# Zeros written in fixed pieces during attention, the first norm ahead of the memsets, a new order of steps, and a join spread over four engines

## The chip, the cores and the metric

The kernel runs on one core of a Trainium2 chip. The core has five engines that run their own instruction streams and wait for each other by semaphores: TensorE (PE, matmuls; PEld is its weight load), VectorE (DVE), ScalarE (ACT), GpSimd (POOL) and SyncE (SP, which here only issues transfers). Sixteen DMA engines carry out the transfers that SP, ACT and POOL issue. The metric is the device time of one execution in microseconds; lower is better.

## The reference

Inputs are x (32 x 112 x 256), a context (32 x 375 x 256) and the weights of one block. What is computed, cut to what matters:

```python
x = x + tanh(g_xattn) * xattn(layernorm(x), ctx, ctx)      # 16 heads of 16, softmax over 375 keys
x = x + tanh(g_ffn) * ffn(layernorm(x))

def ffn(src):
    x = ln(src + attention(src)) * ln1_g + ln1_b           # 16 heads of 16, over 112 keys
    gates = softmax(x @ gW + gb)                            # 8 experts
    top2_scores, top2_idx = top_k(gates, 2)
    h = relu(x @ W1[e] + b1[e]); y = h @ W2[e] + b2[e]      # F = 512
    return ln(x + sum over the top 2 of score * y) * ln2_g + ln2_b
```

There are 32 items of 112 rows, so 3584 rows. Each row goes to two experts.

## The kernel before, in words

The kernel has three phases on the one core.

**Attention** works on 32 items, each through the stages N (norm of x), A (projections of the context and of x), M (maxima of the scores), B (scores, exp, product with the values), F (output, residual, norm), C, X and D (the same three for the self-attention), and E (output, norm, gate, rank, send). A step such as `B.s1` is a part of a stage. The order of all 1414 steps is written out by hand: `FIRST`, then the list `ORDER` once for each turn from `BEGIN` = 8 to `END` = 26, then `LAST`. `Written.run` walks this one program on every engine, and each engine issues only what it has to do for a step, so the lists are the order in each engine's queue. In `ORDER` a suffix such as `-1` or `+3` shifts the item that the step takes in this turn. Steps that need scores or maxima share one PSUM tensor `quad` (depth 1); most others share three `bank`s. The value tensors `values_A` (3 deep) and `values_C` (2 deep) are set to zero and one by VectorE in `prepare()` (step `S.set`) and, for two of them, ahead of the whole program.

SP issues the loads: `N.load` (x of an item, then its context `ctxT`, each after the slot is free, and then weights that are due), `F.load` (x again, for the residual) and `F.shift` (a store to the DRAM tensor `kept`).

**Routing.** `sent` is a DRAM tensor of 8 regions, one for each expert, of `REGION` = 32 x 112 + 128 rows of 258 numbers. `E.rank` finds for each row the next free places in the regions of its two experts (`next_row` is the count), and `E.send` (POOL, two indirect DMAs for an item) writes the rows there. The experts phase reads whole tiles of 128 rows, so the rows behind the last one of a region must be zero. Before, this was done late: after the ranks of item 29 (`LAST_KNOWN`) VectorE copies the counts to `next_i`, SP reads each of the eight with `value_load` and zeroes the 352 rows behind it (`tails_zeroed`), and the sends of items 30 and 31 wait for that.

**Experts.** VectorE makes a table of tiles (`plan_steps`, `table`), and 63 tiles of 128 rows are loaded from `sent`, pass the two matmuls and are scattered to `kept`. This phase begins on SP when `attention_over` (all sends and stores landed) and the table are there. ACT loads the rows kept for the residual to `x1_in`.

**Join.** 28 tiles of 128 rows: SP loads both expert rows of each (`join_in`, 4 slots), PE adds them into PSUM by two products with the identity, DVE takes bn_stats, bn_aggr and the addition of epsilon, POOL the power -0.5 (`join_inv`), DVE the gain (`join_gain`, one buffer) and the product with the inverse deviation plus the residual (`result`), and ACT issues the store. The plan has 8 written-out turns and a loop of 5 passes of 4.

## Time and profile before

| | |
|---|---|
| median of 3 runs | 1215.42 us (1215.26 to 1216.89) |
| the profiled execution | 1216.49 us, its span 1214.7 us |
| PE busy | 1126.1 us, 93% of the span |
| DVE, ACT, POOL busy | 68%, 57%, 22% |
| granted TensorE clock, mean | 0.98 |
| DMA | 79.18 MB in 66597 packets |

The profiled execution is 1.07 us over the median of the runs. The span runs from the first to the last instruction. Attention takes about the first 910 us, the experts until about 1158, the join the rest. In rows of a timeline the first number is the start in us from the start of the span, the second the length in us; "x8" is how many instructions are merged; what stands in brackets is how long the engine was idle before, and what ended that.

### The profile page before, as it was taken

Reading aid. Unit: us, or ns where it says so; the run is one execution under the profiler, and the core shown is the slowest. Engines: PE = TensorE matmul, PEld = TensorE weight load, DVE = VectorE, ACT = ScalarE, POOL = GpSimd, SP = SyncE. Lnnn points to the kernel's source line nnn. Section 1 sums busy time; section 2 is a strip of 40 time slices with the busy share of each in tenths; the row PEclk is TensorE's granted clock in tenths of the full one; section 3 lists DMA queues with packets and bytes.
Section 4 is the critical chain, followed back from the end, with each engine's and each line's share of the span. In section 5 each row is a group of like instructions: output and inputs, shape, how many; then the busy total and the mean of one; then the engine's idle time right before and its main releaser. Section 6 shows DMA issues by size and latency. Waiting matters only on the chain.

```text
span 1214.7 us, 36448 instructions
## 1 busy us (share of the span) xinstructions
PE 1126.1 (93%) x12924; PEld 840.5 (69%) x12925; DVE 827.8 (68%) x2431; ACT 688.4 (57%) x1186; POOL 265.8 (22%) x371
## 2 busy tenths in 40 slices
PE   6999999999999999999999999999728999999964
PEld 4576766676766666676666677667517999999942
DVE  5565777776777777667777776777744666666667
ACT  4666767677666667777667776776513333333200
POOL 1011111122212111222212221222321222222233
PEclk9999999999999999999999999999968999999988
DMA  6012043222111111111111011101056222222165
GB/s 149 22 42 68 17 123 105 69 68 74 40 33 37 51 34 33 38 41 34 33 53 38 10 45 46 30 28 64 28 116 187 71 69 71 72 72 71 52 212 159
DMA packets 66597, 79.18 MB, mean 65 GB/s; under 512 B 14008, under 2 KB 52536, under 8 KB 66328
## 3 DMA queue, kind: packets, MB, share of 16 engines
q1 hardware_dynamic: 52680, 54.24, 16.2%
q0 software_dynamic: 6096, 15.66, 3.9%
q10 hardware_dynamic: 7680, 7.34, 1.9%
q8 instruction: 95, 1.56, 0.6%
q14 instruction: 46, 0.38, 0.1%
HBM read 51.32 MB, written 25.90 MB: 64 GB/s over the span
## 4 chain that ended last, share of the span: by engine, by line
PE 75%; issue 9%; DVE 8%; ACT 4%; POOL 1%; DMA 1%; DVEq 0%; another core or an unknown queue 0%; SPq 0%; POOLq 0%; ACTq 0%
PE quad L1299 11%; PE bank L1289 10%; PE bank L1485 9%; PE quad L1497 9%; PE quad L1311 8%; PE sums L1322 6%; PE bank L1436 4%; PE bank L1389 4%; ACT probs L777 4%; PE quad L1308 3%; PE bank L1282 3%; PE bank L1457 2%; PE bank L1322 2%; DVE row_max_C L1050 2%; DVE row_max_C L1047 2%
## 5 line engine op out<-in xcount | busy, mean ns | idle before, releaser
L777 ACT ACTIVATE probs<-quad 125x1792 f32<-125x1792 f32 (+1 forms) x128 | 213.0, 1664 | 116.9 <-PE quad L1311 116.7
L855 ACT ACTIVATE scored_half<-quad 112x750 bf16<-112x750 f32 (+1 forms) x160 | 131.4, 821 | 89.5 <-PE quad L1299 89.0
L1037 DVE TENSOR_REDUCE row_max_A<-quad 112x2 f32<-112x750 f32 x128 | 120.1, 938 | 70.0 <-PE quad L1299 66.5
L1485 PE MATMUL bank<-tile_inT,tile_w 128*128 128x128 f32 x1008 | 124.4, 277 | 0.3 <-ACT tile_w L887 0.3
L1039 DVE TENSOR_REDUCE row_max_A<-scored_half 112x2 f32<-112x750 bf16 x128 | 118.6, 927 | 3.2 <-ACT scored_half L855 1.0
L1485 PEld LDWEIGHTS bank<-tile_inT,tile_w 128*128 128x128 f32 x1008 | 119.0, 194 | 0.7 <-ACT tile_w L887 0.7
L1497 PE MATMUL quad<-output_w,hiddenT 128*128 x504 | 119.1, 380 | 0.0
L1299 PE MATMUL quad<-kT_A,qT_A 32*112 32x375 f32 x1024 | 115.2, 519 | 3.5 <-ACT probs L777 1.5
L1216 DVE TENSOR_SCALAR hiddenT<-bank,hidden_b 128x128 f32<-128x128 f32 x252 | 71.0, 344 | 63.0 <-PE bank L1485 62.6
L1289 PE MATMUL bank<-ctxT,wxk 128*128 128x375 f32 x256 | 99.1, 510 | 5.5 <-DMA bxk<-in_bxk_dram 5.5
L739 POOL DMA_INDIRECT kept_dram<-tile_out,take_back x63 | 60.4, 959 | 186.3 <-DVE tile_out L1239 179.7
L1497 PEld LDWEIGHTS quad<-output_w,hiddenT 128*128 128x128 f32 x504 | 90.9, 190 | 10.0 <-issue 0.2
L1389 PE MATMUL bank<-wxv,ctxT 128*125 128x256 f32 x384 | 95.5, 385 | 0.0
L1322 PE MATMUL sums<-probs,values_A 125*32 125x112 f32 x3072 | 92.5, 261 | 0.4 <-issue 0.4
L684 POOL TENSOR_TENSOR inv_std_N<-moments_N,minus_half 112x1 f32<-112x1 f32 x32 | 17.6, 549 | 333.9 <-DVE moments_N L945 333.9
L1311 PE MATMUL quad<-qT_A,kT_A 32*125 32x224 f32 x1536 | 88.8, 347 | 0.0
L725 POOL DMA_INDIRECT sent_dram<-xm,send_row x64 | 61.7, 964 | 104.5 <-DVE send_row L1108 47.3
L1322 PEld LDWEIGHTS sums<-probs,values_A 125*32 125x32 f32 x3072 | 72.0, 109 | 14.1 <-issue 9.0
L1389 PEld LDWEIGHTS bank<-wxv,ctxT 128*125 128x125 f32 x384 | 69.1, 189 | 14.8 <-issue 5.1
L1311 PEld LDWEIGHTS quad<-qT_A,kT_A 32*125 32x125 f32 x1536 | 73.0, 183 | 0.0
L1289 PEld LDWEIGHTS bank<-ctxT,wxk 128*128 128x128 f32 x256 | 44.8, 194 | 37.4 <-issue 21.6
L887 ACT ACTIVATE tile_w<-hidden_w 128x1024 f32 x63 | 66.1, 1049 | 0.0
(225 smaller groups left out, 1995.0 us busy)
## 6 DMA issues: line engine op xcount, KB each, us to landing
ctxT<-in_ctxT_dram SPq DMA_DIRECT2D x32, 375.0 KB, 3.5
tile_in<-sent_dram SPq DMA_DIRECT2D x63, 129.0 KB
join_in<-kept_dram SPq DMA_DIRECT2D x28, 256.0 KB, 3.4
hidden_w<-in_hidden_w_dram SPq DMA_DIRECT2D x8, 512.0 KB, 5.0
output_w<-in_output_w_dram SPq DMA_DIRECT2D x8, 512.0 KB, 5.7
x_in<-in_x_dram SPq DMA_DIRECT2D x32, 112.0 KB, 2.9
x_res<-in_x_dram SPq DMA_DIRECT2D x32, 112.0 KB, 3.2
kept_dram<-x_shift SPq DMA_DIRECT2D x32, 112.0 KB
```

Source lines behind the costliest of these rows:

```text
L777: act.activation(probs[0:rows, t.buffer("probs", step), :, :], quad[0:rows, :, 0:U * T], ACT.Exp, scale=SCALE).then_inc(taken[kind_of(step ...
L855: act.activation(scored_half[:, t.buffer("half", step), 0:RT // 2 * n].rearrange("t (r s) -> t r s", s=n), quad[0:T, RT // 2:RT, 0:n], ACT ...
L1037: dve.tensor_reduce(row_max["A"][:, i:P // 2:ROWS], quad[0:T, 0:RT // 2, 0:S], AX_X, ALU.max).then_inc(taken[kind], 1)
L1039: dve.tensor_reduce(row_max["A"][:, P // 2 + i:P:ROWS], scored_half[:, t.buffer("half", step), 0:RT // 2 * S].rearrange("t (r s) -> t r s" ...
L1216: ins = dve.tensor_scalar(hiddenT[:, k, f, :], hidden_bank[k][:, f * P:(f + 1) * P], hidden_b[:, f, bass.ds(e, 1)], 0.0, ALU.add, ALU.max)
L1289: mm = pe.matmul(out, w[:, c, m * P:(m + 1) * P], actT[:, c, :], start=c == 0, stop=c == DC - 1)
L1299: mm = pe.matmul(quad[0:T, i, at:at + n], qT[a][rows, k, c, e, :], kT[a][rows, k, c, :], start=True, stop=True)
L1311: mm = pe.matmul(quad[0:n, i, c * RH * T:(c + 1) * RH * T], kT[a][rows, k, c, j * n:(j + 1) * n], qT[a][rows, k, c, :, :].rearrange("p e t ...
L1322: mm = pe.matmul(out[h * VW:(h + 1) * VW, g * T:(g + 1) * T], values[a][0:n, k, j, g * G + h, :], probs[0:n, b, i, (c * RH + e) * T:(c * R ...
L1389: mm = pe.matmul(bank[0:SC, (j - first) * D:(j - first + 1) * D], ctxT[:, k, c, j * SC:(j + 1) * SC], wxv[:, c, :], start=c == 0, stop=c = ...
L1485: mm = pe.matmul(hidden_bank[k][:, f * P:(f + 1) * P], tile_w[:, k, c, f * P:(f + 1) * P], tile_inT[:, k, c, :], start=c == 0, stop=c == D ...
L1497: mm = pe.matmul(output_bank[k][:, 0:D], hiddenT[:, k, f, :], output_w[:, f, bass.ds(e * D, D)], start=f == 0, stop=f == FC - 1)
```

## The change

1. **The zeros.** `next_i`, the late zeroing and its wait are gone. SP zeroes all regions in 33 fixed pieces of 112 rows (the last of 128), the same rows of all eight regions at once, in two DMAs each. The pieces go out behind the loads of `N.load` from item 4 on, one or two with each. A send of item n waits until piece n + 1 has landed (the last one until all have).
2. **The first norm.** All memsets of the value rings stand in `prepare()`, and in `FIRST` the step `N.ln` of item 0 stands ahead of `S.set`. The bias `bxk` is loaded ahead of `wxk`.
3. **The order.** `ORDER`, `FIRST` and `LAST` are new. In `ORDER`, `N.load` stands without `+3`, and `F.load` with `+1`.
4. **The join.** The plan is written out for all 28 turns. DVE keeps bn_stats, bn_aggr, the gain (`join_gain` now 4 deep) and one addition of epsilon for two tiles; POOL does one power for two tiles and adds the residual to the result; ACT multiplies by the inverse deviation (`ACT.Copy` with a scale) and stores. `result` is 8 deep. POOL, not DVE, waits for `x1_loaded`.

The steps from X.max to E.aT and from D.s to B.s2 in `ORDER`, before and after (| is the end of a turn):

```
before: ... X.max A.q E.send-2 E.oN A.v0 F.norm-1 E.aT ...   ... D.s | A.k0 M.mT-1 B.s2-1 ...
after:  ... X.max A.q E.oN A.v0 X.mT E.send-1 E.aT ...   ... D.s A.k0+1 E.gate F.load+1 M.mT E.pick B.s2 ...
```

```diff
@@ -46,8 +46,7 @@
 REGION = NB * T + P
 
 
-LAST_KNOWN = NB - 3
-BEHIND = (NB - 1 - LAST_KNOWN) * T + P
+FIRST_CLEAR = 4
 NT = NB * T * TOP // P + E - 1
 
 
@@ -176,48 +175,48 @@
 PROBS = 4
 
 ORDER = [
-    "A.k0", "M.mT-1", "B.s2-1", "D.pv-1", "E.gate-1", "B.pv1-1", "N.ln-1", "E.pick-1", "E.rank-1", "B.pv2-1",
-    "E.copy-2", "B.s0", "A.k1", "F.oN", "A.xT", "X.max", "A.q", "E.send-2", "E.oN", "A.v0", "F.norm-1", "E.aT",
-    "M.max0", "F.aT", "F.res", "E.out", "B.s1", "F.out", "A.v1", "M.max1", "F.shift-1", "C.yT", "B.pv0", "N.load+3",
-    "M.max2", "F.load+3", "C.qk0", "X.mT", "M.max3", "C.qk1", "C.bias-1", "C.v", "E.norm", "D.s"]
+    "F.shift-1", "N.ln-1", "B.pv2-1", "B.s0", "F.oN", "A.xT", "F.norm-1", "A.k1", "X.max", "A.q", "E.oN", "A.v0",
+    "X.mT", "E.send-1", "E.aT", "M.max0", "C.bias-1", "F.aT", "E.out", "B.s1", "F.out", "A.v1", "M.max1", "C.yT",
+    "N.load", "B.pv0", "M.max2", "C.qk0", "C.v", "M.max3", "E.norm", "C.qk1", "F.res+1", "D.s", "A.k0+1", "E.gate",
+    "F.load+1", "M.mT", "E.pick", "B.s2", "E.rank", "E.copy", "D.pv", "B.pv1"]
...
 FIRST = """
-    A.k0 A.xT S.set A.k1 A.q A.v0 N.ln S.mask N.ln M.max0 A.k0 M.max1 M.max2 A.v1 A.xT M.max3 A.k1 A.q N.load M.mT
...
+    A.k0 A.xT N.load N.ln S.mask S.set A.k1 A.q A.k0 N.ln M.max0 M.max1 A.xT A.k1 N.load M.max2 A.q M.max3 A.v0
...
@@ -241,9 +240,11 @@
 JT = NB * T // P
 JR = 4
 
-JOIN = Plan(JT, 8, JR, {"A": 0, "B": 1}, ["A.add", "B.norm"], {})
+RR = 8
+
+JOIN = Plan(JT, JT, 1, {"A": 0, "G": 1, "V": 1, "R": 3, "S": 4}, ["A.add", "G.gain", "V.power", "R.scale", "S.store"], {})
 X1_PARTS = 4
-assert JT % X1_PARTS == 0
+assert JT % X1_PARTS == 0 and JT % 2 == 0
 
@@ -557,15 +556,6 @@
                         keys_over(sp)
                         sp.dma_start(output_b[:, :], io["output_b"].rearrange("e d -> (e d)").partition_broadcast(P)
                                      ).then_inc(output_b_loaded, DMA)
-                    elif step == "E.rank" and t.item("E") == LAST_KNOWN:
-
-                        sp.wait_ge(rows_zeroed, 5)
-                        sp.wait_ge(rows_known, 1)
-                        for e in range(E):
-                            row_no = sp.value_load(next_i[0:1, e:e + 1], min_val=e * REGION, max_val=e * REGION + (LAST_KNOWN + 1) * T)
-                            sp.dma_start(io["sent"][bass.ds(row_no, BEHIND), :].rearrange("(p r) (h d) -> p (r h) d", r=4, h=2),
-                                         zero_row[0:BEHIND // 4, :].unsqueeze(1).to_broadcast([BEHIND // 4, 8, SENT // 2])
-                                         ).then_inc(tails_zeroed, DMA)
                     elif step == "F.shift":
                         n, k = t.item("F"), t.slot("F")
                         sp.wait_ge(shifted, t.item("F", 1, 1))
@@ -573,8 +563,8 @@
 
             def load_weights(stage):
                 if stage == "K":
+                    column(bxk, io["bxk"]).then_inc(w_loaded["K"], DMA)
                     square(wxk, io["wxk"]).then_inc(w_loaded["K"], DMA)
-                    column(bxk, io["bxk"]).then_inc(w_loaded["K"], DMA)
                 if stage == "Q":
                     square(wxq, io["wxq"]).then_inc(w_loaded["Q"], DMA)
                     column(bxq, io["bxq"]).then_inc(w_loaded["Q"], DMA)
@@ -597,11 +587,25 @@
                         row(b, io[a]).then_inc(w_loaded["C"], DMA)
                     sp.dma_start(gate_w[:, :, :], io["gate_w"].rearrange("(c p) e -> p c e", p=P)).then_inc(w_loaded["C"], DMA)
 
+            def clear(j):
+
+                rows = T if j < NB else REGION - NB * T
+                regions = io["sent"][:, :].rearrange("(e r) d -> r e d", e=E)
+                for half in (slice(0, SENT // 2), slice(SENT // 2, SENT)):
+                    sp.dma_start(regions[j * T:j * T + rows, :, half],
+                                 zero_row[0:rows, :].unsqueeze(1).to_broadcast([rows, E, SENT // 2])).then_inc(regions_zeroed, DMA)
+
             def turn(t):
                 move(t)
                 n = t.item("N")
                 if t.only != "N.load":
                     return
+                if n == FIRST_CLEAR:
+                    sp.wait_ge(rows_zeroed, 5)
+                if n >= FIRST_CLEAR:
+                    cleared = [(NB + 1) * m // (NB - FIRST_CLEAR) for m in (n - FIRST_CLEAR, n - FIRST_CLEAR + 1)]
+                    for j in range(*cleared):
+                        clear(j)
                 for stage in ("KQV", "BC")[n] if n < 2 else ():
                     load_weights(stage)
                 if n == 6:
@@ -719,8 +723,7 @@
                         pool.wait_ge(xm_copied, t.item("E", 1, 1))
                         pool.wait_ge(row_steps, t.item("E", 6, 6))
                         settled(pool, passed_pool)
-                        if t.item("E") > LAST_KNOWN:
-                            pool.wait_ge(tails_zeroed, E * DMA)
+                        pool.wait_ge(regions_zeroed, (t.item("E") + 1 if t.item("E") < NB - 1 else NB + 1) * 2 * DMA)
                         for i in range(TOP):
                             pool.indirect_dma_start(out=io["sent"], out_offset=bass.IndirectOffsetOnAxis(
                                 ap=send_row[:, k, i:i + 1], axis=0), in_=xm[:, k, i, :], in_offset=None).then_inc(sent[k], DMA)
@@ -740,15 +743,21 @@
                         ap=take_back[:, k, :], axis=0), in_=tile_out[:, k, :], in_offset=None).then_inc(out_stored[k], DMA)
 
             EXPERTS.run(pool, expert_turn)
+            pool.wait_ge(x1_loaded, X1_PARTS * DMA)
 
             def join_turn(t):
-                if t.active("B"):
-                    k = t.slot("B", JR)
-                    pool.wait_ge(join_steady, t.item("B", 1, 1))
-                    if t.later("B", JR):
-                        pool.wait_ge(result_steps, t.item("B", 2, 2 - 2 * JR))
-                    pool.tensor_tensor(join_inv[:, k, :], join_moments[:, k, 1:2], minus_half[:, :],
-                                       ALU.pow).then_inc(join_inverted, 1)
+                if t.active("V") and t.item("V") % 2:
+                    n, k = t.item("V"), t.slot("V", JR)
+                    pool.wait_ge(join_steady, n // 2 + 1)
+                    if t.later("V", JR):
+                        pool.wait_ge(join_scaled, n - JR + 1)
+                    pool.tensor_tensor(join_inv[:, k - 1:k + 1, :], join_moments[:, k - 1:k + 1, 1:2],
+                                       minus_half[:, :].unsqueeze(1).to_broadcast([P, 2, 1]), ALU.pow).then_inc(join_inverted, 1)
+                if t.active("R"):
+                    n, k = t.item("R"), t.slot("R", RR)
+                    pool.wait_ge(join_scaled, n + 1)
+                    pool.tensor_tensor(result[:, k, :], result[:, k, :], x1_in[:, n * D:(n + 1) * D],
+                                       ALU.add).then_inc(join_summed, 1)
 
             JOIN.run(pool, join_turn)
 
@@ -894,20 +903,29 @@
             EXPERTS.run(act, expert_turn)
 
             def join_turn(t):
-                if t.active("B"):
-                    n, k = t.item("B"), t.slot("B", JR)
-                    act.wait_ge(result_steps, t.item("B", 2, 2))
-                    act.dma_start(io["out"][bass.ds(n * P, P), :], result[:, k, :]).then_inc(result_stored[k], DMA)
+                if t.active("R"):
+                    n, k = t.item("R"), t.slot("R", RR)
+                    act.wait_ge(join_inverted, n // 2 + 1)
+                    act.wait_ge(join_gained, n + 1)
+                    if t.later("R", RR):
+                        act.wait_ge(result_stored[k], t.dmas("R", 0, depth=RR))
+                    act.activation(result[:, k, :], join_gain[:, t.slot("R", JR), :], ACT.Copy,
+                                   scale=join_inv[:, t.slot("R", JR), :]).then_inc(join_scaled, 1)
+                if t.active("S"):
+                    n, k = t.item("S"), t.slot("S", RR)
+                    act.wait_ge(join_summed, n + 1)
+                    act.dma_start(io["out"][n * P:(n + 1) * P, :], result[:, k, :]).then_inc(result_stored[k], DMA)
 
             JOIN.run(act, join_turn)
-            for k in range(JR):
-                act.wait_ge(result_stored[k], JT // JR * DMA)
+            for k in range(RR):
+                act.wait_ge(result_stored[k], (JT - k + RR - 1) // RR * DMA)
 
         @block.vector
         def _(dve):
             def prepare():
 
-                dve.memset(values["A"][:, DEEP["A"] - 1, :, :, :], 0.0).then_inc(vset, 1)
+                for i in range(DEEP["A"]):
+                    dve.memset(values["A"][:, i, :, :, :], 0.0).then_inc(vset, 1)
                 for k in range(DEEP["C"]):
                     dve.memset(values["C"][:, k, :, :, :], 0.0).then_inc(vset, 1)
                 dve.wait_ge(vset, DEEP["A"] + DEEP["C"])
@@ -1106,8 +1124,6 @@
                         dve.tensor_reduce(route[:, 0:TOP], rows_pick[:, :, :], AX_X, ALU.add).then_inc(row_steps, 1)
                         dve.wait_ge(row_steps, t.item("E", 6, 5))
                         dve.tensor_copy(send_row[:, k, :], route[:, 0:TOP]).then_inc(row_steps, 1)
-                        if t.item("E") == LAST_KNOWN:
-                            dve.tensor_copy(next_i[:, :], next_row[:, :]).then_inc(rows_known, 1)
                     elif step == "F.out":
                         dve.wait_ge(made["F.out"], t.count(step))
                         dve.wait_ge(res_shifted, t.item("F", 1, 1))
@@ -1160,8 +1176,6 @@
                         dve.scalar_tensor_tensor(xm[:, k, 0, 0:D], r_gain[:, :], inv_std["E"][:, :], ln1_b[0:T, :],
                                                  ALU.mult, ALU.add).then_inc(gained, 1)
 
-            for i in range(DEEP["A"] - 1):
-                dve.memset(values["A"][:, i, :, :, :], 0.0).then_inc(vset, 1)
             ATTENTION.run(dve, turn)
             keys_over(dve)
 
@@ -1240,36 +1254,30 @@
 
             EXPERTS.run(dve, expert_turn)
 
-            dve.wait_ge(x1_loaded, X1_PARTS * DMA)
-
             def join_turn(t):
-                a, b = t.active("A"), t.active("B")
-                kA, kB = t.slot("A", JR), t.slot("B", JR)
-                if a:
-                    dve.wait_ge(join_added, t.item("A", 1, 1))
+                n, k = t.item("A"), t.slot("A", JR)
+                if t.active("A"):
+                    dve.wait_ge(join_added, n + 1)
                     if t.later("A", 2):
-                        dve.wait_ge(join_measured, t.item("A", 2, -2))
-                    dve.bn_stats(join_stats[:, t.slot("A"), :], join_bank[kA][:, 0:D]).then_inc(join_measured, 1)
-                if b:
-                    if t.later("B", 1):
-                        dve.wait_ge(result_steps, t.item("B", 2))
-                    dve.scalar_tensor_tensor(join_gain[:, :], join_bank[kB][:, 0:D], join_moments[:, kB, 0:1], ln2_gain[:, :],
-                                             ALU.subtract, ALU.mult).then_inc(result_steps, 1)
-                if a:
-                    dve.wait_ge(join_measured, t.item("A", 2, 1))
+                        dve.wait_ge(join_measured, 2 * n - 2)
+                    dve.bn_stats(join_stats[:, t.slot("A"), :], join_bank[k][:, 0:D]).then_inc(join_measured, 1)
+                if t.active("G"):
+                    m, km = t.item("G"), t.slot("G", JR)
+                    dve.wait_ge(join_measured, 2 * m + 2)
+                    if t.later("G", JR):
+                        dve.wait_ge(join_scaled, m - JR + 1)
+                    dve.scalar_tensor_tensor(join_gain[:, km, :], join_bank[km][:, 0:D], join_moments[:, km, 0:1], ln2_gain[:, :],
+                                             ALU.subtract, ALU.mult).then_inc(join_gained, 1)
+                if t.active("A"):
+                    dve.wait_ge(join_measured, 2 * n + 1)
                     if t.later("A", JR):
-                        dve.wait_ge(result_steps, t.item("A", 2, 2 - 2 * JR))
-                    settled(dve, passed_dve)
-                    dve.bn_aggr(join_moments[:, kA, :], join_stats[:, t.slot("A"), :]).then_inc(join_measured, 1)
-                    dve.wait_ge(join_measured, t.item("A", 2, 2))
-                    dve.tensor_scalar(join_moments[:, kA, 1:2], join_moments[:, kA, 1:2], TOP * TOP * EPS, None, ALU.add).then_inc(join_steady, 1)
-                if b:
-                    dve.wait_ge(result_steps, t.item("B", 2, 1))
-                    dve.wait_ge(join_inverted, t.item("B", 1, 1))
-                    if t.later("B", JR):
-                        dve.wait_ge(result_stored[kB], t.dmas("B", 0, depth=JR))
-                    dve.scalar_tensor_tensor(result[:, kB, :], join_gain[:, :], join_inv[:, kB, :], x1_in[:, bass.ds(t.item("B", D), D)],
-                                             ALU.mult, ALU.add).then_inc(result_steps, 1)
+                        dve.wait_ge(join_gained, n - JR + 1)
+                        dve.wait_ge(join_inverted, (n - JR) // 2 + 1)
+                    dve.bn_aggr(join_moments[:, k, :], join_stats[:, t.slot("A"), :]).then_inc(join_measured, 1)
+                    if n % 2:
+                        dve.wait_ge(join_measured, 2 * n + 2)
+                        dve.tensor_scalar(join_moments[:, k - 1:k + 1, 1:2], join_moments[:, k - 1:k + 1, 1:2], TOP * TOP * EPS, None,
+                                          ALU.add).then_inc(join_steady, 1)
 
             JOIN.run(dve, join_turn)
 
```

The rest of the diff declares the tensors and semaphores that these lines name, drops `next_i` and its copy and the memsets after `prepare()`, moves all `values_A` memsets into `prepare()`, and lets PE wait for `join_gained` before it reuses a bank in the join.

## Rows read from the trace of the kernel before

**Rows 1.** Windows: us, busy us (instructions) by engine, granted clock, DMA share, GB/s.
```profile
0.00:25.00 25.00, 16.48 (x70) 9.55 (x72) 14.57 (x35) 8.97 (x18) 3.91 (x26) 1.00 0.71 157
400.00:500.00 100.00, 98.22 (x1314) 69.12 (x1313) 70.90 (x199) 70.03 (x122) 22.45 (x32) 1.00 0.12 34
850.00:900.00 50.00, 29.96 (x381) 21.67 (x380) 36.24 (x157) 20.75 (x52) 13.25 (x18) 0.87 0.31 69
900.00:940.00 40.00, 24.04 (x156) 21.71 (x157) 12.05 (x45) 9.24 (x14) 7.67 (x8) 0.74 0.56 164
```

**Rows 2.** Timeline of the head: start, length, engine, line, operation, idle before.
```profile
1.17 1.34 DVE L1164 MEMSET values_A<- 125x1536 f32 x1 [1.04 <-PEq L1536]
...
5.50 2.84 PE L1289 MATMUL bank<-ctxT,wxk 128*128 128x375 f32 x4 [5.50 <-DMA bxk<-in_bxk_dram]
...
10.30 0.63 PE L1282 MATMUL bank<-ident,x_norm 112*128 112x112 f32 x2 [1.96 <-DVE x_norm L950]
...
18.34 0.94 DVE L1037 TENSOR_REDUCE row_max_A<-quad 112x2 f32<-112x750 f32 x1 [5.28 <-PE quad L1299]
```

**Rows 3.** Waits of PE, 100 to 840 us: total, times, longest.
```profile
PE quad L1308 <- ACT probs L777: 4.3, 18, 0.3
PE bank L1282 <- DVE att_E L962: 3.9, 18, 0.4
```

**Rows 4.** Timeline of the seam between attention and experts.
```profile
878.43 22.21 SPq L566 DMA_DIRECT2D sent_dram<-zero_row  x8
...
897.35 0.17 DVE L1108 CAST send_row<-route 112x2 uint32<-112x2 f32 x1
...
900.34 0.28 DVE L1203 CAST table<-bank 1x126 int32<-1x126 f32 x1 [0.46 <-PE bank L1464]
...
905.96 0.98 POOL L725 DMA_INDIRECT sent_dram<-xm,send_row  x1 [11.90 <-DMA sent_dram<-zero_row]
...
909.73 0.94 POOL L725 DMA_INDIRECT sent_dram<-xm,send_row  x1 [0.30 <-issue]
913.35 29.20 SPq L631 DMA_DIRECT2D tile_in<-sent_dram  x11
```

**Rows 5.** Windows of the join: written-out turns, then the loop.
```profile
1168.30:1175.46 7.16, 5.19 (x22) 3.45 (x20) 6.99 (x27) 0.00 (x0) 3.69 (x6) 1.00 0.97 315
1175.46:1203.80 28.34, 19.43 (x70) 12.05 (x71) 24.67 (x85) 0.00 (x0) 11.27 (x18) 1.00 0.77 230
```

**Rows 6.** Timeline of the join: tile 3's turn, and the end.
```profile
1168.30 0.42 DVE L1252 BATCH_NORM_STATS2 join_stats<-sums 128x6 f32<-128x256 f32 x1
...
1168.64 0.47 DVE L1256 SCALAR_TENSOR_TENSOR join_gain<-bank,join_moments,ln_gain 128x256 f32<-128x256 f32 x1
1169.03 0.17 DVE L1263 BATCH_NORM_AGGREGATE join_moments<-join_stats 128x2 f32<-128x6 f32 x1
1169.23 0.15 DVE L1265 TENSOR_SCALAR join_moments<-join_moments 128x1 f32<-128x1 f32 x1
1169.31 0.49 DVE L1271 SCALAR_TENSOR_TENSOR result<-join_gain,join_inv,x_in 128x256 f32<-128x256 f32 x1
1169.46 0.74 POOL L750 TENSOR_TENSOR join_inv<-join_moments,minus_half 128x1 f32<-128x1 f32 x1 [0.67 <-DVE join_moments L1265]
...
1207.38 0.42 DVE L1252 BATCH_NORM_STATS2 join_stats<-sums 128x6 f32<-128x256 f32 x1
...
1209.57 0.49 DVE L1271 SCALAR_TENSOR_TENSOR result<-join_gain,join_inv,x_in 128x256 f32<-128x256 f32 x1
```

**Rows 7.** DMA queues, 876 to 906 us: packets, MB, share of 16 engines.
```profile
q1 hardware_dynamic: 5848, 3.02, 48.9%
```

**Rows 8.** DMA issues of the page: count, KB each, us to landing.
```profile
ctxT<-in_ctxT_dram SPq DMA_DIRECT2D x32, 375.0 KB, 3.5
```

**Rows 9.** Groups by line and shape, GpSimd and ScalarE: count, busy, mean ns.
```profile
L714 POOL TENSOR_TENSOR y_bias<-y,bso 112x256 f32<-112x256 f32 x32 | 23.4, 732 | 10.0 <-DVE y L950 10.0
...
L841 ACT ACTIVATE xm<-xm 112x256 f32<-112x256 f32 x32 | 13.0, 410 | 4.8 <-DVE xm L1160 4.8
```

82 lines of the change are left out of this document (40 added, 42 removed).

## The prediction

> **What bounds the kernel now.** I read the windows first: busy time of each engine in stretches that follow the stages. In the middle of attention TensorE is busy 98.22 of 100 us at the full clock, no other engine over 71 [rows 1]: there TensorE's work sets the pace, and an edit can win only the 1.8% between its instructions. TensorE stands idle at three places: 8.5 us in the first 25; the end of attention with the start of the experts, where 850 to 940 us hold 54 us of work, 36 idle [rows 1]; and the join, where it waits for VectorE. So I read the timeline of those three, and the waits of TensorE for the stretch between.
>
> *Head.* TensorE starts at 5.50, when the bias bxk lands, needs 2.84 us for the first keys, and then waits 1.96 for x_norm: VectorE had begun with the memsets of the value rings at 1.17, and the first norm stood behind them [rows 2].
>
> *Middle.* Two waits make up most of its gaps, each once in each of the 18 written-out turns: 4.3 us for the probabilities and 3.9 for att_E [rows 3].
>
> *Seam to the experts.* The last rows to send are known at 897.35, and the table at 900.62. But GpSimd's send waits 11.90 us for the zeros behind the rows, whose eight DMAs SyncE issues from 878.43 to 900.64, each after reading its place from next_i; four sends then run from 905.96 to 910.67 and the first expert tile is fetched at 913.35 [rows 4]. The wait lies on the chain.
>
> *Join.* VectorE is busy 6.99 of 7.16 us in the written-out turns, while the DMA engines are at 0.97 and move 315 GB/s [rows 5]. One turn is five instructions, 0.42, 0.47, 0.17, 0.15 and 0.49 us long [rows 6]. In the loop the turn is longer: tile 3's bn_stats starts at 1168.30 and tile 27's at 1207.38, 39.08/24 = 1.63 us a tile, with DMA at 0.77 and 230 GB/s [rows 5, 6].
>
> **The change, part by part.** *1. The tails' zeroing goes away.* Sends then wait for pieces zeroed long before: piece n+1 leaves with an input load some four turns ahead of send n. The two sends of tile 31 need send_row (897.35 + 0.17); with one handoff they start near 897.7 and, at the spacing of the four, (909.73 - 905.96)/3 = 1.26 us [rows 4], the last starts at 898.96 instead of 909.73: **-10.8**. Tile 30's two sends, ready at about 890, fit in before. Next late is the table at 900.62; the last send lands by 898.96 + (913.35 - 909.73) = 902.6, so the table costs nothing. Bounds: -9.5 if table and a queue for GpSimd cost 1.3 more, -11.3 with nothing between.
>
> *2. The zeros during attention.* 33 pieces, two DMAs each, 896 runs of 516 bytes in each. Before, 5,632 such packets made up nearly all of 5,848 on that queue, which took 48.9% of 16 engines' 30 us: 235/5848 = 40 ns each [rows 7]. A piece is 1,792 x 40 ns / 16 = 4.5 us of all engines, about one in a turn of 27 us, while the DMA share there is 0.12 [rows 1]. SyncE issues eight of 704 runs in 22 us with the reads between [rows 4], so at most 2.8 us for each, 6 to 7 us a turn, after the turn's own loads. Behind the zeros stand F.load, F.shift and the next N.load. In the 18 turns these have over 10 us of spare TensorE work ahead of their use, by counting the steps between. In the hand-written end there is less: the context of item 26 and the x of item 30 leave about one landing (3.5 us for ctxT [rows 8]) before use. I take **+1** for it, bounds 0 and +6 (one piece, 4.5, and a part of a second ahead of such a load).
>
> *3. First norm ahead of the memsets.* x_norm is then ready before the first keys are done: the 1.96 us go. But the memsets now stand ahead of M.max0, which VectorE did at 18.34 after being idle 5.28 [rows 2]; the work that moved is longer than that idleness by little. bxk issued before wxk only swaps which lands last. **-1.5**, bounds 0 and -3.
>
> *4. The new order.* Between D.s and the next B.s2 stand the same two steps (A.k0, M.mT) in both, so the 4.3 us stay. Between E.oN and E.aT the new order puts X.mT as well, 0.25 us of TensorE, against a wait of 3.9/18 = 0.22 a turn: up to -3.9 [rows 3]. FIRST and LAST leave a little less work between some users of the one quad (M.max, B.s); by counting, 1 to 2 us more. After B.pv2 of the last item, both orders hold nearly the same steps, so the chain to the last send stays as long. **-2.0**; all the 8.2 us of waits are too much, so the bounds are -5 and, for a tight place that I don't see, +5.
>
> *5. The join.* VectorE loses the last product (0.49) and half of the small additions (0.15 each); from start to start in rows 6, bn_stats to gain takes 0.34, gain to bn_aggr 0.39, bn_aggr 0.17 and a handoff, and every second turn the addition with its wait, 0.28 at most: about 1.05 a tile. ScalarE gets a scaling like its copy of 112x256, 0.41, and the store. GpSimd gets the addition of 112x256, 0.73 [rows 9], and one power for two tiles, 0.74 [rows 6]: (0.74 + 2 x 0.73)/2 = 1.1, with three handoffs of 0.1 to 0.15 some 1.25. The DMA engines move 256 KB in and 128 KB out for a tile, 393 kB: at 315/0.97 = 325 GB/s that is 1.21 us, at 230/0.77 = 299 it is 1.31 [rows 5]. So the bound passes from VectorE to the DMA engines and GpSimd together: 1.28 a tile, 24 x (1.63 - 1.28) = -8.4. The end gets longer: one result now passes power, two scalings, an addition on GpSimd and the store. From tile 27's bn_stats to its store it was 2.7 us; it is 0.34 + 0.39 + 0.2 + 0.2 for VectorE, 0.85 for the power, 0.9 for two scalings, 0.85 for the sum, 3.9 with handoffs: +1.2. **-7.2**; bounds: at 1.21 a tile -8.9, at 1.57 (below) +0.3.
>
> In rows 6 the power on GpSimd takes 0.74 while a product with two SBUF inputs runs on VectorE, and the new join has no such product left. The Trainium skill (SBUF — State Buffer, "SBUF: two separate sides") says that GpSimd and VectorE lock their shared pair exclusively when VectorE has two SBUF inputs or a 2-port mode; by it the new additions are disturbed less. The Trainium skill (GPSIMD Engine Reference, "Performance versus the Vector engine") also holds that an addition of two tensors is 1.96 times VectorE's; on VectorE's product of 0.47 that would be an estimate of 0.92 for one, 1.3 us a tile for GpSimd and -6.6 for this part; the row has 0.73.
>
> **Sum.** -10.8 + 1.0 - 1.5 - 2.0 - 7.2 = -20.5 us. The profiled execution took 1216.49, so 1196.0; it is 1.07 over the median of the runs, so **1195** against 1215.42.
>
> **Rivals.**
> - *The join gains nothing*: GpSimd becomes its bound. If each addition is held by VectorE's gain (0.47), a pair is 0.74 + 2 x (0.73 + 0.47) = 3.1, 1.57 a tile, 24 x 0.06 = 1.4 less 1.2 for the end: 1202. For it: GpSimd's power, a single column, takes 0.74 beside VectorE's products [rows 6]. Against: the 0.73 is measured in attention, with VectorE at 71% [rows 1, 9]. 15%.
> - *Everything works*: the order wins its 3.9 and more, head -3, join at 1.21: 1188. 15%.
> - *Order or zeros cost*: a tight place in the 18 turns, 0.3 us each (+5), or GpSimd and VectorE held by a late load near item 30: 1200 to 1204. 10%.
> - *The other side, slower than before*: the zeros delay loads in every turn. N.load stands in its own turn now, no longer three ahead, and waits in SyncE's queue behind F.shift and the zeros before. Were TensorE held in each of the 28 loads, the change turns slower from 20.5/28 = 0.73 us each; by a full piece (4.5 us) it would be 1215.4 - 21.5 + 126 = 1320. Against: the load leaves about a turn before use, and ctxT lands 3.5 us after issue [rows 8]. 5%, of which 2 for a delay that just eats the gain.
> - *The zeros weren't on the chain* (something else ends at 910): the wait of 11.90 names them, and SyncE's reads end at 900.64; 1206. 4%.
>
> **How the numbers follow.** 51% for 1195 with its own range 1191 to 1199; with the rivals at 1188 and 1202 on the two sides, 1187 to 1205 leaves out the 5%, the 4% and the ends of the others. Within 0.2% (2.4 us, about what a measurement of this kernel can tell from no change) 2%; slower 3%; faster 95%.
>
> **What the profile after would show.** No wait of GpSimd for zeros near 900, and the first tile_in about 3.5 us after the last send_row plus two sends, near 902.6 on the old time base (some 3 us earlier by head and order). The wait of 1.96 for x_norm gone. In the middle TensorE at 98.2 to 98.6 of 100 and DMA share 0.28 to 0.34 instead of 0.12. In the join, bn_stats of tiles 3 and 27 about 30.7 us apart, VectorE busy near 80%, DMA share over 0.9, GpSimd over 80%. Wrong would be: a wait of TensorE or VectorE for ctxT or x_in; a turn longer than before; a join at 1.4 us and more, with the additions over 0.9 us.

## The result, and the profile after

The changed kernel took **1222.55 us** (median of 20 runs, 1216.11 to 1233.85) against 1215.10 us (20 runs, 1213.66 to 1216.89) of the kernel before beside it: ratio 1.0062, 95% interval 1.0044 to 1.0080. That is slower by 0.6%; I had predicted 1195 us. Its profiled execution took 1223.01 us, with a span of 1220.8. Its line numbers are 3 to 18 higher than before. Of the experiments further down, one of the four runs of long_runs_again was slow (1604.64 us, mean granted clock 0.65): the median in its row holds it, its ratio does not.

First the two ends, since they came out nearly as predicted. The seam, timeline, against [rows 4]:

```profile
918.68 0.17 DVE L1126 CAST send_row<-route 112x2 uint32<-112x2 f32 x1
919.67 0.94 POOL L728 DMA_INDIRECT sent_dram<-xm,send_row  x1 [1.90 <-DVE send_row L1126]
920.91 0.94 POOL L728 DMA_INDIRECT sent_dram<-xm,send_row  x1 [0.30 <-issue]
921.76 0.28 DVE L1217 CAST table<-bank 1x126 int32<-1x126 f32 x1 [0.46 <-PE bank L1472]
924.62 1.52 SPq L635 DMA_DIRECT2D tile_in<-sent_dram  x2
```

From the last send_row to the first expert tile it is now 924.62 - 918.68 = 5.94 us, before 913.35 - 897.35 = 16.00: -10.06. The wait for the zeros is gone. The join, against [rows 5, 6], the bn_stats of tiles 3 and 27 and a window between:

```profile
1180.34 0.43 DVE L1263 BATCH_NORM_STATS2 join_stats<-sums 128x6 f32<-128x256 f32 x1 [0.22 <-PE sums L1519]
...
1210.76 0.43 DVE L1263 BATCH_NORM_STATS2 join_stats<-sums 128x6 f32<-128x256 f32 x1
```

```profile
1185.00:1205.00 20.00, 15.27 (x62) 10.42 (x61) 14.49 (x54) 8.12 (x16) 16.53 (x25) 1.00 0.96 310
```

24 tiles take 30.42 us instead of 39.08. VectorE is busy 72% of the time and GpSimd 83%; the DMA share is 0.96. So the bound did pass to the transfers, with GpSimd close behind. From tile 27 to the end it is 10.04 us, before 7.32.

But the last send_row comes at 918.68, not at 897.35: all that the ends won was lost, and more, before it. The windows, against [rows 1] (in the two stretches from 100 to 300, which have no row there, TensorE was busy 98.60 and 98.15 of 100 us before):

```profile
0.00:25.00 25.00, 16.33 (x70) 8.74 (x72) 14.46 (x35) 9.25 (x20) 3.91 (x26) 0.93 0.71 160
100.00:200.00 100.00, 92.27 (x1232) 64.33 (x1231) 69.04 (x170) 65.19 (x111) 18.11 (x26) 0.97 0.59 112
200.00:300.00 100.00, 92.46 (x1146) 65.50 (x1147) 61.66 (x163) 62.25 (x108) 19.11 (x27) 0.93 0.54 106
400.00:500.00 100.00, 99.30 (x1296) 69.87 (x1293) 73.50 (x186) 71.29 (x127) 23.05 (x32) 1.00 0.34 72
```

Where nothing disturbs it, as from 400 to 500, TensorE is busy 99.3 of 100 us, better than I forecast (98.2 to 98.6). From 100 to 300 it is idle 15 us, and the granted clock is 0.97 and 0.93. The waits of TensorE from 100 to 840 us, against [rows 3]:

```profile
PE sums L1330 <- issue: 9.5, 3, 4.2
PE quad L1307 <- ACT probs L786: 5.3, 4, 3.0
PE quad L1316 <- ACT probs L786: 4.2, 18, 0.2
PE quad L1319 <- issue: 2.5, 1, 2.5
```

The wait for att_E is gone, and the 4.2 us for the probabilities are there as predicted. New are waits for "issue": time in which the engine stood still, though nothing that the profile shows was missing. One of them, in the timeline of TensorE, falls into the middle of a group of 16 matmuls with the same inputs:

```profile
261.65 0.72 PE L1319 MATMUL quad<-qT_A,kT_A 32*125 32x224 f32 x9
...
264.83 1.12 PE L1319 MATMUL quad<-qT_A,kT_A 32*125 32x224 f32 x7 [2.46 <-issue]
```

No operand can be late between the ninth and the tenth. Another one, at 507, stops two engines at once, with the windows around it:

```profile
510.98 1.66 ACT L786 ACTIVATE probs<-quad 125x1792 f32<-125x1792 f32 x1 [3.82 <-remote]
511.04 0.26 DVE L978 RECIPROCAL inv_sum_F<-bank 112x16 f32<-112x16 f32 x1 [3.98 <-remote]
...
512.70 1.05 PE L1307 MATMUL quad<-kT_C,qT_C 32*112 32x112 f32 x32 [3.00 <-ACT probs L786]
```

```profile
503.00:506.00 3.00, 3.00 (x106) 2.50 (x102) 2.37 (x13) 2.63 (x7) 0.00 (x0) 1.00 1.24 139
506.00:509.00 3.00, 3.00 (x53) 2.29 (x44) 0.41 (x1) 0.80 (x2) 2.46 (x4) 1.00 1.24 186
509.00:512.00 3.00, 0.69 (x3) 0.09 (x1) 0.93 (x3) 1.02 (x1) 1.26 (x2) 1.00 0.40 91
512.00:515.00 3.00, 2.31 (x39) 2.20 (x40) 1.26 (x3) 2.27 (x4) 0.00 (x0) 0.83 0.02 5
```

Four DMAs of zeros (two pieces) had been issued together, from 495.97 on. The share of the DMA engines is 1.24 up to 509, and they move only 139 and 186 GB/s, where they moved 310 in the join. ACT and DVE come back 2 us after the share begins to fall, at 509. The granted clock then is 0.83 in the mean of the next window, that is, the lower level, 1.2 GHz, for a part of it: the idle stretch costs twice. From 100 to 840 us the clock is at the lower level for 23.8 us in all, in the trace of late_zeros_third below never. In these 740 us the waits for issue add up to 14.2 us and the waits of L1307 for the probabilities to 4.8 more than there; the 23.8 us at half the clock cost up to 11.9 more, an estimate. The other long turns lie at the same kinds of places: where a piece leaves with 1 MB of expert weights (items 6 to 13), or where two pieces leave together.

The page's DMA queues, against 66597 packets and a queue q1 of 16.2% before:

```profile
q1 hardware_dynamic: 107408, 81.99, 32.7%
...
q8 instruction: 96, 1.57, 0.6%
```

### The profile page after: what moved, and what is told of

It reads as the page before. It is cut to its first block, busy times and chain, and to the rows that moved or that the text cites. A ratio compares the mean times of both kernels' runs of the same rounds, so it can differ in the third digit from the quotient of the medians.

```text
span 1220.8 us, 36170 instructions
## 1 busy us (share of the span) xinstructions
PE 1134.5 (93%) x12924; PEld 849.9 (70%) x12925; DVE 821.4 (67%) x2388; ACT 707.8 (58%) x1214; POOL 276.9 (23%) x385
## 3 DMA queue, kind: packets, MB, share of 16 engines
q1 hardware_dynamic: 107408, 81.99, 32.7%
q8 instruction: 96, 1.57, 0.6%
## 4 chain that ended last, share of the span: by engine, by line
PE 85%; ACT 4%; issue 4%; DMA 2%; DVE 2%; POOL 1%; another core or an unknown queue 1%; SPq 0%; POOLq 0%; DVEq 0%; ACTq 0%
PE bank L1297 12%; PE quad L1307 11%; PE bank L1493 9%; PE quad L1505 9%; PE quad L1319 8%; PE bank L1397 7%; PE sums L1330 7%; PE bank L1444 5%; PE quad L1316 4%; ACT probs L786 3%; PE bank L1290 3%; PE bank L1433 3%; PE bank L1465 2%; PE bank L1330 2%; DMA join_in<-kept_dram 2%
## 5 line engine op out<-in xcount | busy, mean ns | idle before, releaser
L1307 PE MATMUL quad<-kT_A,qT_A 32*112 32x375 f32 x1024 | 115.7, 521 | 5.6 <-DVE row_max_A L1055 4.4
L1319 PE MATMUL quad<-qT_A,kT_A 32*125 32x224 f32 x1536 | 91.6, 355 | 2.5 <-issue 2.5
L688 POOL TENSOR_TENSOR inv_std_E<-moments_E,minus_half 112x1 f32<-112x1 f32 x32 | 18.8, 589 | 235.1 <-DVE moments_E L963 234.9
```

The costliest lines, as they stand in the source:

```text
L1307: mm = pe.matmul(quad[0:T, i, at:at + n], qT[a][rows, k, c, e, :], kT[a][rows, k, c, :], start=True, stop=True)
L1319: mm = pe.matmul(quad[0:n, i, c * RH * T:(c + 1) * RH * T], kT[a][rows, k, c, j * n:(j + 1) * n], qT[a][rows, k, c, :, :].rearrange("p e t ...
```

## The experiments

My theory after this (A): the bursts of small packets keep the engines from getting their instructions. Rivals: the new order is slower (B); loads come late behind the zeros (C); the bytes or the total, not the burst of packets, cost (D). The ratio is always to the kernel before on the same chip. It takes 1203.9 us (medians 1203.85 to 1204.34) beside the first, third and fourth group of experiments, and 1216.6 beside the second.

| kernel | us | ratio, 95% interval | kernel before |
|---|---|---|---|
| late_zeros | 1203.59 | 0.9998 (0.9988 to 1.0007) | 1203.89 |
| zeros_in_before | 1214.49 | 1.0089 (1.0072 to 1.0106) | 1203.89 |
| apart | 1212.62 | 1.0071 (1.0055 to 1.0088) | 1203.89 |
| long_runs | 1190.12 | 0.9883 (0.9866 to 0.9899) | 1203.89 |
| after_again | 1220.95 | 1.0041 (1.0027 to 1.0055) | 1216.62 |
| join_only | 1210.20 | 0.9944 (0.9927 to 0.9961) | 1216.62 |
| long_old_order | 1201.97 | 0.9884 (0.9867 to 0.9900) | 1216.62 |
| long_runs_again | 1191.21 | 0.9876 (0.9856 to 0.9896) | 1203.85 |
| late_zeros_again | 1204.12 | 1.0000 (0.9990 to 1.0010) | 1203.85 |
| long_quads | 1205.42 | 1.0013 (0.9995 to 1.0031) | 1203.85 |
| after_third | 1212.22 | 1.0073 (1.0049 to 1.0097) | 1204.34 |
| late_zeros_third | 1204.47 | 1.0002 (0.9993 to 1.0012) | 1204.34 |
| long_runs_third | 1189.83 | 0.9884 (0.9868 to 0.9901) | 1204.34 |
| long_apart | 1196.74 | 0.9936 (0.9913 to 0.9958) | 1204.34 |

**Part 1 undone** (late_zeros): `clear` and its calls out, the late zeroing of the tails back in.

```diff
-                    for j in range(*cleared):
-                        clear(j)
...
+                        for e in range(E):
+                            row_no = sp.value_load(next_i[0:1, e:e + 1], ...)
+                            sp.dma_start(io["sent"][bass.ds(row_no, BEHIND), :]...).then_inc(tails_zeroed, DMA)
```

> The changed kernel with part 1 alone undone: no fixed pieces, the tails zeroed late behind item 29 as before; new order, first norm and join stay. Theory A (the packets of the pieces fill the 16 DMA engines in bursts, and while they do, the engines get no instructions and stop): no turn of 30 us and more, every turn about 26.4 us; the last send_row near 891 to 896 instead of 918.7; GpSimd's wait for the zeros (about 12 us) is back; 1202 to 1206 us. Theory B (the new order of steps is itself slower): the turns of 30 us stay, the last send_row near 915, and with the wait back 1228 to 1235 us. Theory C (loads of data come late behind the zeros): as A in time, since the zeros are gone.

It took 1203.59. All the 18 turns take 26.38 us, and from 100 to 840 us TensorE shows two waits for issue, of 0.6 and 0.2 us; this fits A and C, and B falls as the cause of the stops. The last send_row is at 884.1, 7 us earlier than I had written. The ratio surprised me: 1.000, where the join alone should give 0.995. That question is taken up below.

**Part 1 alone** (zeros_in_before): the same edit the other way round, in the kernel before.

> The kernel before with part 1 alone: fixed pieces behind the loads of N.load, no late zeroing; old order, old head, old join. Theory A: the stops appear in the old order too, about 20 to 26 us in all, and the send wait of 10 to 11 us goes: 1222 to 1232 us. Theory B (the order, not the zeros, costs): attention ends as before and the wait goes: 1203 to 1206 us. Theory C: slower than A or the same, but with waits of TensorE, VectorE or GpSimd for ctxT, x_in or x_res in the profile, not stops without a wait.

Ratio 1.0089: the stops appear in the old order too. From 100 to 840 us TensorE waits 5.6 us for issue at the product with the values (before: 0.4). A again, and C in part, since a wait of 5.1 us for x_norm stands beside it. Part 1 alone makes the kernel slower, though it takes away a wait of 10 us.

**The same pieces, each alone** (apart):

```diff
+                if t.only == "B.pv0":
+                    m = t.item("B")
+                    ...
+                    sp.wait_ge(made["B.pv"], NSC * m + 1)
+                    for j in (m,) if m < NB - 1 else (m, m + 1):
+                        clear(j)
```

> The changed kernel with the same 33 pieces and the same packets, but each piece issued by itself in the middle of a turn (SyncE waits for the first product with the values of the item), so no piece leaves together with another one, or with an input load or the 2 MB of expert weights; only the last two go together. Theory A: the DMA engines are never full for longer than one piece, the stops go: last send_row 893 to 898, 1195 to 1200 us. If total packets or bytes matter and not the burst (theory D): nothing won, 1218 to 1226 us. Theory B: 1218 us and more.

1212.62: the time of A missed, its picture there. Windows of this kernel, its longest waits of TensorE in the first 100 us, and what SyncE issued around the second of them:

```profile
0.00:100.00 100.00, 83.24 (x818) 54.15 (x820) 53.13 (x110) 52.47 (x85) 9.45 (x35) 0.93 0.42 91
100.00:700.00 600.00, 593.67 (x7867) 417.30 (x7866) 447.20 (x1147) 431.62 (x744) 125.81 (x177) 1.00 0.34 85
```

```profile
PE bank L1298 <- DMA ctxT<-in_ctxT_dram: 6.4, 1, 6.4
PE bank L1298 <- DMA wxk<-in_wxk_dram: 6.4, 1, 6.4
```

```profile
43.37 0.96 SPq L595 DMA_DIRECT2D sent_dram<-zero_row  x2
44.38 1.56 SPq L544 DMA_DIRECT2D x_in<-in_x_dram  x1
46.04 1.37 SPq L548 DMA_DIRECT2D ctxT<-in_ctxT_dram  x1
```

From 100 to 700 us, with every piece alone, TensorE is busy 98.9% and no stop is left, at the same number of packets. So the total doesn't cost, the burst does (D falls for the total). What it lost it lost outside the 18 turns, by late loads.

- The wait for wxk is the start of the program, as in the changed kernel (6.15 us there). The wait for ctxT ends at 52.65. SyncE issues the piece only after the first product with the values, so it stood still until 43.30 with the input loads behind it: this ctxT left at 46.04 (in after_third at 35.26) and landed 6.5 us later.
- The turn from 726 to 757 us is 31.3 us long instead of 24.8. There x_in left behind a piece and landed after 7.1 us (2.3 in the changed kernel's page), and VectorE waited 4.4 us for it.
- The last x_res left behind two pieces at 853.59 and landed 9.5 us later; TensorE waited 5.4 us for what comes of it.

That is C, at places where the changed kernel has no such wait and no such piece, and a part of it is not the zeros but the wait that this experiment put into SyncE's queue.

**The same bytes in long runs** (long_runs, three times): the zeros are copied from a small DRAM tensor in 16 runs of 7 KB for each region, one DMA a piece.

```diff
-                for half in (slice(0, SENT // 2), slice(SENT // 2, SENT)):
-                    sp.dma_start(regions[j * T:j * T + rows, :, half],
-                                 zero_row[0:rows, :]...)
+                sp.dma_start(regions[:, j * T:j * T + rows, :].rearrange("e (p q) d -> p e (q d)", p=16),
+                             io["zeros"][0:rows, :].rearrange("(p q) d -> p (q d)", p=16)....to_broadcast([16, E, rows // 16 * SENT]))
```

> The changed kernel with the pieces at their old places, but copied from a DRAM tensor of zeros in 16 runs of 7 KB for each region instead of 896 runs of 516 bytes twice: the same 0.92 MB written for a piece, but one DMA and far fewer packets. Theory A with packets as the price: a piece takes about 3 us of all engines instead of 6, most stops go, 1197 to 1208 us. If bytes fill the engines (theory D for bytes; a copy also reads its bytes from DRAM): the bursts are as long or longer and the time is 1218 to 1230 us.

> The changed kernel with the pieces written in runs of 7 KB, as before 0.988 of a kernel before that took 1203.9. Its own turns were 26.38 us there, as those of the changed kernel are on both chips. So where the kernel before takes 1216 us this should still take about 1190 us: ratio 0.978 to 0.981. If the chip shifts all kernels alike: 0.988 again.

> The changed kernel with the pieces in runs of 7 KB: 0.9883 and 0.9876 of a kernel before of 1203.9 us. Beside one of 1216 us: about 1192 us, 0.979 to 0.982.

All three met a kernel before of 1204 us, so what the second and third forecast say for one of 1216 us was not tested. 0.9883, 0.9876 and 0.9884: faster than the kernel before by 1.2%, and than the changed kernel by 1.9%, with the pieces at their old places. The queue of the third of them, and its TensorE's waits for issue from 100 to 840 us:

```profile
q1 hardware_dynamic: 52000, 82.12, 22.2%
```

```profile
PE sums L1334 <- issue: 1.3, 2, 0.9
```

The bytes are the same (82 MB), the packets half. Two more things differ: the zeros come from DRAM instead of SBUF, and a piece is one DMA instead of two; no run here parts these from the length of the runs. This is the sharpest comparison, since the changed kernel, the one without pieces and this one ran side by side. The start of outT_F of item 31, the last of its kind, is in the changed kernel (after_third), with late zeros, and with long runs:

```profile
866.41 0.54 ACT L875 ACTIVATE outT_F<-sums 128x448 f32<-128x448 f32 x1 [0.17 <-PE sums L1330]
```

```profile
839.60 0.55 ACT L874 ACTIVATE outT_F<-sums 128x448 f32<-128x448 f32 x1 [0.16 <-PE sums L1331]
```

```profile
842.62 0.54 ACT L879 ACTIVATE outT_F<-sums 128x448 f32<-128x448 f32 x1 [0.16 <-PE sums L1334]
```

The pieces cost 26.8 us in small packets and 3.0 in long ones (1.6 in the two other pairs of profiles). Of the 26.8, 1.6 lie ahead of the first piece (outT_F of item 0 is at 49.91 instead of 48.29). From outT_F of item 0 to that of item 31 the three kernels with late zeros take 791.3 to 791.9 us, the three with long runs 793.7 to 794.3, and the three profiles of the changed kernel 809.8, 816.5 and 824.1: 18 to 33 us for small packets, 2 to 3 for long ones.

**Long runs, but bursts of four or five pieces** (long_quads):

> As the runs of 7 KB, but the pieces leave four or five together with every fourth N.load: 3.7 to 4.6 MB at once, so the DMA engines are full for 12 to 18 us at a stretch, longer than any burst in the changed kernel (about 8 us), with few packets. If full DMA engines as such stop the instruction streams, the stops are back, 5 us and more for each of seven bursts: 1215 us and more (or loads come late, which the waits would name). If it is the many small packets, it runs as the kernel with single pieces, within 4 us.

1.0013, between the two forecasts. One of its bursts, windows, and the longest wait of TensorE from 690 to 715 us:

```profile
690.00:706.00 16.00, 12.33 (x188) 9.12 (x186) 7.16 (x22) 9.88 (x20) 0.00 (x0) 0.97 1.01 319
706.00:710.00 4.00, 0.39 (x2) 0.29 (x2) 0.92 (x4) 0.00 (x0) 2.14 (x3) 0.50 0.09 32
```

```profile
PE bank L1294 <- DVE y L972: 7.3, 1, 7.3
```

The waits of TensorE for issue from 100 to 840 us:

```profile
PE sums L1334 <- issue: 3.2, 3, 1.8
PE quad L1311 <- issue: 1.8, 2, 1.3
```

GpSimd's timeline in the burst:

```profile
707.68 0.72 POOL L706 TENSOR_TENSOR x_res<-x_res,bxo 112x256 f32<-112x256 f32 x1 [22.00 <-DMA x_res<-in_x_dram]
```

For 16 us the DMA engines are full at 319 GB/s. TensorE works on for 12 of them without a stop for issue, until GpSimd's x_res is late, and that the profile names. So this burst cost what I had counted, late data. Five turns with other bursts are 0.7 to 2.1 us longer, 5.7 in all, about as much as the waits for issue, which are 5.2 us with one more of 0.2. So full DMA engines with long packets stop the instruction streams too, but for 1.8 us at most, though the bursts are nearly twice as long as those of the changed kernel; its longest stop is 4.2.

**The changed kernel again, beside others** (after_again, after_third):

> The changed kernel, unchanged, beside the same runs of the kernel before as the experiments of this call. Ratio 1.006 as measured before if chips only shift both kernels alike; up to 1.02 if, as the late zeroing (0.9998) suggests, the new order costs some us more on a chip where the kernel before has short turns. The turns of 30 us should be there again, not all at the same items.

> The changed kernel, unchanged, once more. Beside a kernel before of 1216.6 us it was 1.0041 of it. Its own turns without a stop (26.38 us) are the same everywhere, those of the kernel before are 26.36 or 26.75 us. So beside a kernel before of 1204 us I expect about 1.013 to 1.017, beside one of 1216 us again 1.003 to 1.008.

1.0041 and 1.0073, the second under the 1.013 to 1.017 that I had written. The turns of 30 us and more are there each time, not all at the same items, and the runs spread over 12 to 18 us where the kernel before spreads over 1.5 to 3.2. A part of the spread is the clock: the profiled run of after_again, 1210.27 us, has a mean granted clock of 0.979 and not one stretch at the lower level from 23 to 866 us; the five others, 1217.87 to 1222.28 us, have 0.971 to 0.973.

**The join alone** (join_only):

> The kernel before with part 4 alone, the new join: old order, old head, late zeroing. From the two traces, 55.9 us from the first load of the join to the end go to 49.8: -6 us, ratio 0.995. My prediction had -7.2. Rival: the join's gain is paid back elsewhere (the wait for x1_loaded, the code of 28 written-out turns): ratio 0.998 or more.

0.9944 (0.9927 to 0.9961): the join's gain is real, -6.4 us by the medians and -6.8 by the ratio, near the predicted -7.2. So the rival falls.

**Old order, new join, long runs** (long_old_order):

> The kernel before with the new join and the pieces written in runs of 7 KB (part 1 in its cheap form and part 4), old order and old head. If the new order and the first norm win what I predicted (3.5 us), this is slower than the same with the new order (0.9883): 0.991 to 0.992. If they cost some 4 to 6 us, as the late zeroing suggests (0.9998 where the join alone should give 0.995), it is 0.984 or less, and the fastest of all so far.

0.9884, between the two forecasts, and the same ratio as with the new order, but on the chip where the kernel before is slow. The kernel with the new order and long runs was not run on that chip.

**The kernel before, profiled on both kinds of chip** (before_again 1215.13 us, before_third 1203.72 us):

> The kernel before, unchanged, profiled beside the experiments, since the kernel before ran in 1203.9 us beside the first four experiments and in 1215.1 us beside the changed kernel. Open is where the 11 us between the two lie. If they lie in attention (turns of 26.38 us, as in every kernel of the first four experiments, instead of 26.75), the new order wins nothing per turn; if they lie elsewhere and the turns are 26.75, it wins 0.37 us a turn.

> The kernel before, profiled once more beside the kernels of this call. So far the kernel before ran in 1203.9 us beside the first four experiments (no profile of it there) and in 1216.6 us beside the next four, with turns of 26.75 us. If it runs in about 1204 us here, its turns should be about 26.36 us, as those of its copy with the fixed zeros were; if in 1216, again 26.75.

The turns are 26.77 and 26.36 us. Timeline of the same place in a turn, TensorE's scores of item C and VectorE's maximum of them; first where the kernel is slow, then where it is fast:

```profile
623.58 1.05 PE L1299 MATMUL quad<-kT_C,qT_C 32*112 32x112 f32 x32
...
625.23 1.09 DVE L1047 TENSOR_REDUCE row_max_C<-quad 112x8 f32<-112x896 f32 x1 [1.02 <-PE quad L1299]
```

```profile
617.01 1.05 PE L1299 MATMUL quad<-kT_C,qT_C 32*112 32x112 f32 x32
...
618.13 1.09 DVE L1047 TENSOR_REDUCE row_max_C<-quad 112x8 f32<-112x896 f32 x1 [0.49 <-PE quad L1299]
```

On the one chip VectorE starts 0.60 us after the end of the matmuls, on the other 0.07, in the same program. The median over the turns is 0.59 against 0.07. In the old order this delay reaches att_E, for which TensorE then waits 0.2 us in each turn [rows 3]; with the small delay it doesn't wait at all. The new order has X.mT between and takes 26.38 us on either chip. But the delay is no fixed cost of the one chip: in after_again, on the same chip as before_again, its median is 0.07 too. It comes with the old order on that chip alone, and why stays open, as does how much of the 11.4 us between the two profiles it makes; the turns alone are 18 x 0.41 = 7.4. Each chip was measured on one occasion only.

**The late zeros beside the fast kernel before** (again and third):

> The changed kernel with part 1 undone, 0.9998 of a kernel before that took 1203.9. It leaves parts 2, 3 and 4. Where the kernel before takes 1216 us, I expect 1203 to 1205: ratio 0.989 to 0.990, of which the new join is 0.9944, so that the order and the first norm are -5 to -6 us there; where it takes 1204, 0.9998 again, so that they are +5 to +6 us.

> The changed kernel with part 1 undone: 0.9998 and 1.0000 of a kernel before of 1203.9 us. Beside one of 1216 us: 1203 to 1206 us, 0.989 to 0.992, with turns of 26.38 us; if it is 0.9998 there too, the new order brings nothing anywhere.

1.0000 and 1.0002; again no chip with a kernel before of 1216 us was met. The traces of before_third and late_zeros_again, from the same chip, say where the join's gain went. The last send_row is at 884.31 and 883.81: order and first norm together win 0.5 us. But the late zeroing starts with the rank of item 29, and in the new `LAST` that rank comes later: SyncE's eight DMAs begin at 871.26 instead of 865.93, and the first expert tile at 904.87 instead of 899.81. These 5.1 us eat most of the join's gain. They belong to the combination of new order and late zeros, not to the change.

**The version that the experiments pointed to** (long_apart): long runs, each piece at `B.pv0` from item 3 on, and wxk ahead of bxk.

> The version that the experiments point to: pieces in runs of 7 KB, each issued in the middle of a turn instead of with the input loads and the weights, and wxk loaded ahead of bxk again. In its trace the kernel with 7 KB runs is 1.6 us behind the one with late zeroing at the last item of attention, and the first matmul starts 0.65 later with bxk first. So 1 to 2 us less than the kernel with 7 KB runs, 1188 to 1190 us; no less if those 1.6 us are bytes and not collisions.

0.9936, a miss: it is slower than long_runs. At the last outT_F it is only 1 us behind (843.57), at the last send_row 6.3. Between the two GpSimd waits 13.0 us for the last x_res, which SyncE issues at 837.44 behind two pieces, in long_runs_third at 824.55: a late load again. The best version stays long_runs, 0.988 of the kernel before.

## Why the prediction was wrong, step by step

*Tails (-10.8):* right, -10.06. *Join (-7.2):* right in mechanism and nearly in size: tiles 3 to 27 30.42 us apart where I had 30.7; the end was mis-sized, +2.7 instead of +1.2, together -5.9 in the trace and -6.4 us by the medians of join_only. VectorE is busy 72% instead of near 80. The upper bound had a wrong sign: at 1.57 a tile the sum is 1.2 - 1.4 = -0.2, not +0.3. GpSimd's addition takes 0.71 us in the join. The Trainium skill (GPSIMD Engine Reference, "Performance versus the Vector engine") has such an addition at 1.96 times VectorE's; by the estimate of 0.92 that the prediction drew from it a pair would have held GpSimd for 1.3 us a tile. The trace has 0.71, and decides. Much of the miss lies in where I applied the ratio, VectorE's three-operand product (0.47). VectorE's own addition of 112x256 (r, with one input in PSUM) takes 0.41 us in this trace and GpSimd's 0.73, 1.8 times, near the page's 1.96.

*First norm (-1.5):* the wait of 1.96 us is gone, x_norm's product starts at 8.79 right behind the first keys. But the keys start at 6.15 instead of 5.50 [rows 2], now behind wxk, and VectorE's maximum is late for the next scores by 2.09 us. In the first 25 us TensorE is busy 16.33 us, before 16.48, and the granted clock is 0.93 instead of 1.00: nothing won there.

*Order (-2.0, bounds -5 and +5):* mis-sized, on the good side. On the chip of this prediction's profile an undisturbed turn is 0.37 us shorter, more than the 0.22 of the att_E wait; over 18 turns that is 6.7 us, past my bound of -5. On the others a turn is 0.02 longer, and order and first norm together win 0.5 us. What both won in the measured run no experiment shows, since late_zeros was never run on a chip where the kernel before is slow. A gain over my bound is luck here: I had priced the wait and not what lies around it.

*Zeros (+1, bounds 0 and +6):* **the step that failed.** Against the kernel without them they cost 26.8 us of attention on the one chip where both were profiled, where I had put +1. That alone is more than the whole forecast gain of 20.5. I divided the packets' time by 16 engines, 4.5 us a piece and "about one in a turn of 27 us", and then asked only which data loads stand behind them, and whether these have spare work ahead of their use. They had, as counted: from 100 to 840 us the changed kernel shows a single wait for a load (GpSimd for x_res, 12.3 us, which is 11.3 us long with late zeros too) and none of TensorE, and with long runs the pieces cost 1.6 to 3.0 us. Two things I left out. First, a mean over a turn is not the burst: one or two pieces leave together with the input load and, for items 6 to 13, 1 MB of weights, and in the two bursts that I looked at (193 to 202 and 500 to 509 us) the share is above 1.2 for 9 us. Second, the data loads are not the only transfers: the page of the profile lists two queues named "instruction" (96 + 46 packets), which no load of the kernel uses and for which I had no term. The packets also took longer than the 40 ns of [rows 7]: q1 went from 52680 packets and 16.2% to 107408 and 32.7%, so 0.327 x 16 x 1220.8 - 0.162 x 16 x 1214.7 = 3239 us for 54728 more, 59 ns each, with what they slowed the others by.

The rival "the zeros delay loads every turn" had the right place and the wrong mechanism: its test, a wait for ctxT or x_in, would have cleared the zeros, while they cost over 20 us and TensorE's waits in the middle name no load.

What is shown: the loss comes from the zeros and from bursts of them, not from the new order (zeros_in_before, late_zeros) and not from their total number (apart). With the same bytes written in long runs nearly all of it goes; that it is the length of the runs, and not the source in DRAM or the single DMA, is the nearest reading but was not tested apart.

What is not shown by an experiment is that it is the fetch of instructions that starves; none moved the fetches themselves. The traces support it, though. Engines stop between two instructions of one group, and two of them resume within 0.06 us of each other. In the four stops I looked at, one transfer of the instruction queue q8 lies in the stop and lands 0.5 to 2.0 us before the engine comes back. Such a transfer comes about every 9 us all through attention, so this alone would be weak. But its place can be counted. Every kernel with the new order has 96 of them, 16384 bytes each, and in the three traces with late zeros the same one starts after the same number of TensorE's matmuls, within 28 of them (from one to the next it is 122 in the mean): they follow the instruction stream, as the queue's name says. Against the median of these three, 15 transfers of the changed kernel between 100 and 840 us start 30 or more matmuls too late, up to 133. Those at its five longest stops (117, 198, 231, 262 and 509 us) are 59, 98, 114, 133 and 83 late. The two other profiles of this kernel have 15 each as well, with long runs there are 4 in each of three traces (69 at most), with pieces alone 4 (52 at most), in long_apart 6 (100 at most), and in long_quads 8, its one stop of 1.8 us right behind one that is 98 late. Against it: three other transfers in the changed kernel (294, 322 and 671 us) are 83 to 115 late with no stop of over 1.5 us behind them, and being late together with a full DMA line is not yet being the cause.
